# A two-layer perceiver kernel: masked keys of the first cross attention replaced by the mean of their block's unmasked keys, in place of mask products on the scores

## The chip, the cores and the metric

One core of one Trainium2 chip runs the whole program. The metric is device time in microseconds (us); the time before is 1705.82 us, the median of 3 runs (1701.45 to 1709.58).

## The reference, cut to what matters

Two layers, each of cross attention to a long context, self attention, and a mixture of experts. The change touches the first cross attention alone:

```python
q = _ln(q, qn_w, qn_b) * scale            # heads of 32 features, 16 heads, 512 queries
k = _ln(k, kn_w, kn_b)                    # 8192 keys
attn = jnp.einsum('bihd,bjhd->bhij', q, k)
attn = jnp.where(padding_mask[:, None, None, :], attn, -jnp.inf)
p = jax.nn.softmax(attn, axis=-1)
ctx = jnp.einsum('bhij,bjhd->bihd', p, v).reshape(b, s1, c)
```

The padding mask is true for a stretch at the end of the 8192 keys, so most blocks of 512 keys are wholly masked. With these inputs four of the sixteen blocks have unmasked keys (128 row maxima of 32 for each block in the trace), and only these are computed.

## The kernel before, in words

An attention has two halves. The first (`row_maxima`, lines 434 to 1183) goes over the active blocks, computes keys, values and scores, and keeps only the maximum of each row of scores for each head; keys and values are saved to DRAM. The second (`weighted_values`) computes the scores again, this time with the maximum subtracted, and the weighted values. A mask has to keep a masked key from winning a maximum in the first half, and from getting weight in the second. The change is to the first half of the first cross attention (`norm` and `whole` are true there, and nowhere else).

Its work on one block, for TensorE, is 16 *quads*, k = 0 to 15: one for each chunk c of four heads and each tile q of 128 queries. `quad` (L681 on) writes the scores of the four heads, 128 queries by 512 keys each, into two pairs of PSUM banks (`half` 0 and 1; a pair is two heads), by four products of 32 rows (L695) that lie in different row groups of the array. Then four products of 4 rows (L706) add the key mask: `PICK` is a matrix of ones in one row of each group, `KEYROW` holds 0 or -1e30 for each key, made by `key_bias` (L1049) at the head of the block. After the quad come two of the 32 products of the next block's keys (`project_keys`, L628) and this block's values (`project_values`, L670). In the last block there are only the values, one product for each quad, and no `spread`. (The trace counts each fp32 product twice.)

VectorE reduces each pair to two maxima (L1079, `tensor_reduce` of 128x1024), which frees it. There are three pairs, so that half h of a quad has to wait until the pair written three halves before has been reduced: the second half of a quad waits for the first half of the quad before. VectorE also normalises the keys of the next block: `invert` (L1025) takes reciprocals of the deviations, two after quad 9 and two after quad 10; TensorE spreads them over the heads' rows (`spread`, L681, after quad 11); `scale` (L1032) multiplies the keys `KW` by them, and ScalarE's `finish_keys` (L859) applies weight and bias of the norm and writes `KF`. `variances` (L649) stands after quad 8.

The queues are written out by hand, and every engine runs its own in order. ScalarE, near the end of a block (L949 to L956): values 0 and 1, `finish_keys` for chunks 0, 1, 2, values 2, four squares of a count of the second cross attention's mask (L836), values 3, `finish_keys` for chunk 3. SyncE, in `body` (L578 on), begins a block with `load_counted`, four loads of 1 MB of that second mask (L577), then `load_mask(i + 1)`, the key mask of the next block (L528, one 64 KB load, `KM`), then context and saves:

```python
wait_alone(sp, bias_ready, i + 1 + B)
load_mask(i + 1)
```

Each engine crosses from one block to the next through a loop with branches. GpSimd has nothing to do in this half but clear tiles for the second.

Of the kernel before, what the change touches and what calls it, by code (L numbers as in the profile page):

```python
# [14 lines left out]
P = 128  # L15
# [176 lines left out]
def active_blocks(nc, m, tag, count):  # L192
# [7 lines left out]
    class Parts:  # L200
        listed, listed_at = steps_done, 10
        weights, vectors, x = weights_loaded, vectors_loaded, x_loaded
# [12 lines left out]
        @staticmethod  # L215
        def vector(dve):
            v = nc.vector
            v.memset(m.CTL[:, :], 0).then_inc(steps_done, 1)
            v.memset(m.MINUS1[:, :], -1.0).then_inc(steps_done, 1)
            v.memset(m.ONEB[:, :], 1.0).then_inc(steps_done, 1)  # L220
            dve.wait_ge(keys_known, 16)
            v.tensor_reduce(F, m.KM[0:NB, 0:KB], AX.X, ALU.max).then_inc(steps_done, 1)
            dve.wait_ge(steps_done, 4)
            v.tensor_scalar(F, F, 0.0, None, ALU.is_gt).then_inc(steps_done, 1)
            dve.wait_ge(loaded, 16)
            v.tensor_copy(m.IDB[:, :], m.ident[:, :]).then_inc(steps_done, 1)
            v.tensor_copy(m.PICK[:, :], m.pick.to_broadcast([P, P])).then_inc(steps_done, 1)
            dve.wait_ge(products_done, 1)
            v.tensor_copy(POS, m.bank[2][0:NB, 0:1]).then_inc(steps_done, 1)
            dve.wait_ge(steps_done, 8)  # L230
# [4 lines left out]
            dve.wait_ge(steps_done, 10)  # L235

        @staticmethod
        def tensor(pe):
            t = nc.tensor
            pe.wait_ge(loaded, 16)  # L240
            pe.wait_ge(steps_done, 5)
            t.matmul(m.bank[2][0:NB, 0:1], m.upto[0:NB, 0:NB], F, start=True, stop=True).then_inc(products_done, 1)
            pe.wait_ge(steps_done, 9)
            t.matmul(m.bank[3][0:1, 0:1], m.ones[0:NB, 0:1], F, start=True, stop=True)
            t.matmul(m.bank[3][0:1, 1:1 + NB], m.index[0:NB, 0:1], LST, start=True, stop=True).then_inc(products_done, 1)
# [182 lines left out]
def row_maxima(nc, m, L):  # L428
# [25 lines left out]
    squared, inverse_ready, keys_final = m.sem(n + "_sq", norm), m.sem(n + "_rstd", norm), m.sem(n + "_kfull", dyn)  # L454
    maxima_done, mask_summed = m.sem(n + "_block", whole), m.sem(n + "_summed", L.row_mask)
    first_context = [m.sem(f"{n}_ctx_first{d}", norm) for d in range(DC)]
    values_stored = [m.sem(f"{n}_vstored{kb}", dyn) for kb in range(KT_)]
# [18 lines left out]

    VAR_AFTER, INVERSE_AFTER, SPREAD_AFTER = 8, (9, 10), 11

# [34 lines left out]
    class Parts:  # L513
        @staticmethod
        def sync(sp):
# [63 lines left out]
            def body(i):  # L579
                if counting:  # L580
                    load_counted(i)
                with sp.If(i + 1 < nb):
                    wait_alone(sp, bias_ready, i + 1 + B)
                    load_mask(i + 1)
# [23 lines left out]
        def tensor(pe):  # L608
# [65 lines left out]
            def spread(j, before, at):  # L674

                pe.wait_ge(inverse_ready, j * 4 + 4 + B)
                for half in range(2):
# [7 lines left out]
            def quad(i, at, k):  # L685
# [5 lines left out]
                for half in range(2):  # L691
                    pe.wait_ge(scores_taken, first_pair(i) + max(0, 2 * at - 2 + half))
                    for e in range(2):
                        g = 2 * half + e
                        last = t.matmul(m.pair[(2 * at + half) % 3][:, e, k0:k1], QF[rows(g), c, q * P:(q + 1) * P],  # L695
                                        m.KF[rows(g), c, k0:k1], start=True, stop=not whole)
                    if not whole:
                        last.then_inc(scores_ready, 1)
                if not whole:
                    return  # L700
                if k == 0:
                    pe.wait_ge(bias_ready, i + 1 + B)
                for half in range(2):
                    for e in range(2):
                        g = 2 * half + e
                        last = t.matmul(m.pair[(2 * at + half) % 3][:, e, :], m.PICK[rows(g, 4), :], m.KEYROW[rows(g, 4), :],  # L706
                                        start=False, stop=True)
                    last.then_inc(scores_ready, 1)
# [75 lines left out]
            if norm:  # L784

                pe.wait_ge(inverse_ready, 4 + B)
                for half in range(2):
# [38 lines left out]
        def scalar(act, at_last):  # L826
# [71 lines left out]
            if not begun:  # L898
# [29 lines left out]
            def body(i):  # L928
# [8 lines left out]
                with act.If(i + 1 < nb):  # L937
# [37 lines left out]
        def gpsimd(pool):  # L975
            g = nc.gpsimd
            if S:
                pool.wait_ge(q_projected, DC)
# [26 lines left out]
            if not norm:  # L1005

                def body(i):
                    with pool.If(i + 1 < nb):
                        copy_keys(i + 1, i)

                active_loop(pool, nb, body)
            return nb

        @staticmethod
        def vector(dve, at_last):
# [17 lines left out]

# [22 lines left out]
            def maxima(i, ahead):  # L1056
                if L.row_mask:
                    with dve.If(i >= 1):
                        row_bias(i)
                    dve.wait_ge(bias_ready, i + 1 + B)  # L1060
                elif dyn:
                    with dve.If(i >= 1):
                        key_bias(i)
                    dve.wait_ge(bias_ready, i + 1 + B)
                else:
                    dve.wait_ge(mask_loaded, 16)
                for at, k in enumerate(order if ahead else range(NS)):
                    if k == "spread":
                        scale(first_pair(i), at)
                        continue  # L1070
# [60 lines left out]

            if norm:
                for part in range(4):
                    invert(0, part)
# [5 lines left out]

                for half in range(2):
                    dve.wait_ge(scores_ready, B + half + 1)
                    s = m.KW[:, 2 * half:2 * half + 2, :]
                    v.tensor_tensor(s, s, m.pair[1 + half], ALU.mult).then_inc(scores_taken, 1)
                invert_query(0)
                scale_query(0)
                scale_query(1)
                key_bias(0)
                invert_query(2)
# [1026 lines left out]
def build(nc, d, out):  # L2176
    with ExitStack() as ctx:
# [43 lines left out]
        m.MASK = sb("MASK", [P, 2, NQ, KB])  # L2221
        m.MI, m.MB = m.MASK[:, 0].bitcast(I32), m.MASK[:, 1]
        m.MBK = m.BIG[:, 5 * DC * KB:5 * DC * KB + KT_ * T // 2].bitcast(BF16).rearrange("p (b n) -> p b n", n=T)

# [5 lines left out]
        m.CON, m.VT = sb("CON", [P, len(CONST), P]), sb("VT", [P, len(VEC), 4])  # L2230
        m.IDB, m.ONEB, m.PICK = (sb(x, [P, P], BF16) for x in ("IDB", "ONEB", "PICK"))
        m.KMW, m.KBIAS = sb("KM", [P, KB // 4], I32), sb("KBIAS", [P, KT_])
# [100 lines left out]
```

## Time and profile before

| what | value |
|---|---|
| median of 3 runs | 1705.82 us |
| lowest, highest run | 1701.45, 1709.58 us |
| profiled execution: its own time, read as its span | 1710.0 us |
| TensorE busy | 1608.9 us, 94% |
| VectorE busy | 1028.7 us, 60% |
| ScalarE busy | 522.1 us, 31% |
| GpSimd busy | 100.3 us, 6% |
| mean granted TensorE clock | 0.974 of full |
| first half of the first cross attention, by first score product of each block | 53.66, 116.46, 174.80, 231.97 us; ends at 277.62 us |

No time beyond the span is given for the profiled execution. Busy shares are means over stages with different limits. PE is TensorE (PEld its weight loads), DVE VectorE, ACT ScalarE, POOL GpSimd, SPq the queue of SyncE that issues DMAs.

### The profile page before, as it was taken

Reading aid. Unit: us, or ns where it says so; the run is one execution under the profiler, and the core shown is the slowest. Engines: PE = TensorE matmul, PEld = TensorE weight load, DVE = VectorE, ACT = ScalarE, POOL = GpSimd, SP = SyncE. Lnnn points to the kernel's source line nnn. Section 1 sums busy time; section 2 is a strip of 40 time slices with the busy share of each in tenths; the row PEclk is TensorE's granted clock in tenths of the full one; section 3 lists DMA queues with packets and bytes.
Section 4 is the critical chain, followed back from the end, with each engine's and each line's share of the span. In section 5 each row is a group of like instructions: output and inputs, shape, how many; then the busy total and the mean of one; then the engine's idle time right before and its main releaser. Section 6 shows DMA issues by size and latency. Waiting matters only on the chain. (4 is left out here: it accounts for less than half of the span.)

```text
span 1710.0 us, 27863 instructions
## 1 busy us (share of the span) xinstructions
PE 1608.9 (94%) x9460; PEld 758.6 (44%) x9471; DVE 1028.7 (60%) x1681; ACT 522.1 (31%) x781; POOL 100.3 (6%) x82
## 2 busy tenths in 40 slices
PE   7999999999899889999999899998999899989997
PEld 3333333222343376666665433332222244467775
DVE  6677777999746551111111599998979945652223
ACT  3434434878413310000000211114658612200000
POOL 0200001000002010000000320000300001010001
PEclk9899998999999989999999999998999999989999
DMA  4442332211067967666661423210412021239996
GB/s 167 149 151 110 143 141 82 64 51 37 0 133 124 197 235 256 235 233 225 235 235 57 152 91 117 74 67 32 158 39 74 0 86 32 100 122 336 325 327 228
DMA packets 73420, 240.28 MB, mean 141 GB/s; under 512 B 7328, under 2 KB 20528, under 8 KB 54032
## 3 DMA queue, kind: packets, MB, share of 16 engines
q1 hardware_dynamic: 64752, 220.42, 39.8%
q10 hardware_dynamic: 6048, 10.69, 1.7%
q0 software_dynamic: 2560, 8.39, 1.5%
q8 instruction: 36, 0.59, 0.1%
q14 instruction: 24, 0.20, 0.0%
HBM read 214.04 MB, written 35.91 MB: 146 GB/s over the span
## 5 line engine op out<-in xcount | busy, mean ns | idle before, releaser
L1564 ACT ACTIVATE BIG<-banks 128x1024 f32<-128x1024 f32 (+5 forms) x320 | 282.1, 934 | 122.5 <-PE banks L1510 121.7
L1086 DVE CUSTOM_DVE_ANT_0 BIG<-banks,MASK,MX 128x512 bf16<-128x512 f32 (+5 forms) x384 | 228.9, 656 | 61.8 <-issue 38.3
L2106 PEld LDWEIGHTS banks<-KF,BIG 128*128 128x128 f32 x1792 | 227.0, 191 | 14.1 <-issue 14.1
L2106 PE MATMUL banks<-KF,BIG 128*128 128x160 f32 (+1 forms) x1792 | 229.2, 289 | 2.6 <-DVE KF L1824 2.0
L2134 PE MATMUL banks<-BIG,PB 128*128 128x512 f32 x448 | 202.9, 600 | 0.0
L695 PE MATMUL banks<-KF,XN 32*128 32x512 f32 (+4 forms) x1280 | 188.8, 609 | 11.4 <-DVE MX L1086 3.8
L1503 PE MATMUL banks<-XN,KF 32*128 32x512 f32 (+4 forms) x1280 | 187.9, 614 | 7.4 <-ACT BIG L1564 5.3
L1615 DVE TENSOR_TENSOR PB<-PB,BIG 128x2048 f32<-128x2048 f32 (+5 forms) x78 | 165.7, 2124 | 22.6 <-ACT BIG L1564 20.2
L1079 DVE TENSOR_REDUCE MXW<-banks 128x2 f32<-128x1024 f32 x128 | 150.3, 1216 | 44.6 <-PE banks L706 43.4
L1470 PE MATMUL banks<-BIG,V 128*32 128x512 f32 (+4 forms) x1280 | 160.4, 570 | 5.0 <-issue 2.6
L2134 PEld LDWEIGHTS banks<-BIG,PB 128*128 128x128 f32 x448 | 81.5, 190 | 113.1 <-issue 112.9
L670 PE MATMUL banks<-WV,XNT 128*128 128x512 f32 x256 | 126.2, 617 | 0.0
L695 PEld LDWEIGHTS banks<-KF,XN 32*128 32x128 f32 x1280 | 59.3, 186 | 144.9 <-DVE MX L1086 71.6
L628 PE MATMUL banks<-CT,WK 128*128 128x512 f32 x224 | 115.4, 643 | 4.5 <-DVE WK L420 4.5
L1503 PEld LDWEIGHTS banks<-XN,KF 32*128 32x128 f32 x1280 | 63.7, 187 | 124.9 <-issue 75.4
L2019 ACT ACTIVATE PS<-banks 128x512 f32<-128x512 f32 x20 | 11.9, 597 | 332.7 <-PE banks L2134 299.9
L1893 DVE TENSOR_TENSOR PB<-V,banks 128x640 f32<-128x640 f32 x32 | 26.3, 821 | 118.6 <-ACT V L2005 114.5
L1615 DVE TENSOR_TENSOR PS<-PS,BIG 128x2048 f32<-128x2048 f32 (+5 forms) x39 | 82.9, 2126 | 8.5 <-ACT BIG L1564 7.6
L1888 DVE TENSOR_SCALAR V<-banks 128x512 f32<-128x512 f32 x24 | 16.6, 691 | 115.4 <-PE banks L2106 113.6
L866 ACT ACTIVATE V<-banks 128x512 f32<-128x512 f32 x40 | 23.9, 597 | 197.3 <-PE banks L670 197.3
L1615 DVE TENSOR_TENSOR BIG<-BIG 128x2048 f32<-128x2048 f32 (+5 forms) x39 | 80.4, 2062 | 5.0 <-ACT BIG L1564 4.3
L670 PEld LDWEIGHTS banks<-WV,XNT 128*128 128x128 f32 x256 | 43.7, 189 | 70.1 <-issue 60.5
(296 smaller groups left out, 1468.1 us busy)
## 6 DMA issues: line engine op xcount, KB each, us to landing
BIG<-in_L0f_w SPq DMA_DIRECT2D x64, 1024.0 KB, 4.8
BIG<-in_L1f_w SPq DMA_DIRECT2D x48, 1024.0 KB, 5.7
BIG<-in_mask_q SPq DMA_DIRECT2D x16, 1024.0 KB, 8.0
k_saved<-KF SPq DMA_DIRECT2D x32, 256.0 KB, 2.7
CT<-in_ctx SPq DMA_DIRECT2D x6, 1024.0 KB, 4.8
XNT<-in_ctx SPq DMA_DIRECT2D x6, 1024.0 KB, 6.4
v_saved<-V SPq DMA_DIRECT2D x24, 256.0 KB, 2.4
KF<-k_saved SPq DMA_DIRECT2D x24, 256.0 KB, 3.3
```

The source lines that it names most:

```text
L628: last = t.matmul(bank[:, n0:], m.WK[:, d, x * P:(x + 1) * P], KSRC[:, d, n0:], start=d == 0, stop=d == DC - 1)
L670: last = t.matmul(value_bank(kb), tokens[:, d, kb * P:(kb + 1) * P], m.WV[:, d, :], start=d == 0, stop=d == DC - 1)
L695: last = t.matmul(m.pair[(2 * at + half) % 3][:, e, k0:k1], QF[rows(g), c, q * P:(q + 1) * P], m.KF[rows(g), c, k0:k1], start=True, stop=n ...
L1079: v.tensor_reduce(m.MXW[:, H * q + h:H * q + h + 2], pair, AX.X, ALU.max).then_inc(scores_taken, 1)
L1086: last = v.tensor_tensor_reduce(m.JUNK[:, 2 * half + e, k0:k1], pair[:, e, k0:k1], bias, 1.0, mx, ALU.add, ALU.max, mx)
L1470: last = t.matmul(m.bank[6 + c % 2][rows(g), q0:q1], m.V[:, kt[k], HD * h:HD * h + HD], m.PE_[:, s % NP, g, q0:q1], start=k == 0, stop=k = ...
L1503: t.matmul(out(g), m.KF[rows(g), c, ks], m.QF[rows(g), c, q0:q1], start=not biases, stop=False)
L1564: a.activation(m.PE_[:, s % NP, 2 * half:2 * half + 2, q0:q1], m.pair[(2 * s + half) % 3][:, :, q0:q1], ACT.Exp).then_inc(exp_ready, 1)
L1615: v.tensor_tensor(dst, dst, m.PE_[:, s % NP, :, q0:q1], ALU.add).then_inc(sum_taken, 1)
L1893: v.tensor_tensor(out, ex, hidden[k % 2], ALU.mult).then_inc(hidden_copied, 1)
L2106: last = t.matmul(out, W1[k][:, d, f * P:(f + 1) * P], XE[:, d, :], start=d == 0, stop=d == DC - 1)
L2134: last = t.matmul(YB, HS[:, 4 * k + f, 0:P], W2[k][:, f, :], start=k + f == 0, stop=(k == NF - 1 and f == 3), skip_group_check=True)
```

## The change

In this half a masked key now gets the mean of the unmasked keys of its block as its key. A score against a mean of keys is the mean of their scores, so that it can't exceed their maximum. To get there:

- the deviations' reciprocals are multiplied by the mask (a fifth step of `invert`), so that masked keys come out of `scale` as zeros;
- `scale` is now four `tensor_tensor_reduce` of 128x512, which give the sums of the keys as well, and one small step makes them means;
- GpSimd's `fill_keys` adds (mask) x (mean) to each chunk in two steps with a wait between; `finish_keys` waits for it;
- `key_mask` (after quad 3, for the next block) makes the mask, the count of keys and its reciprocal; it needs the key mask of the next block in SBUF;
- SyncE's wait before `load_mask` is on the fifth inverse; ScalarE's order at the start and at a block's end is changed;
- `key_bias`, `PICK` and the four mask products of each quad go; `scores_ready` is raised after each half's own products.

```diff
@@ row_maxima
+    MASK_AFTER, VAR_AFTER, INVERSE_AFTER, SPREAD_AFTER = 3, 8, (9, 10), 11
+    INVERTED = 5
+    NKEYS, KSUMS, KMEANS = m.small[:, 248:249], m.small[:, 250:250 + DC], m.small[:, 254:254 + DC]
@@ sync, body
                 if counting:
                     load_counted(i)
                 with sp.If(i + 1 < nb):
-                    wait_alone(sp, bias_ready, i + 1 + B)
+                    if whole:
+                        wait_alone(sp, inverse_ready, i * INVERTED + INVERTED + B)
+                    else:
+                        wait_alone(sp, bias_ready, i + 1 + B)
                     load_mask(i + 1)
@@ tensor, spread
-                pe.wait_ge(inverse_ready, j * 4 + 4 + B)
+                pe.wait_ge(inverse_ready, j * INVERTED + INVERTED + B)
@@ tensor, quad
                         last = t.matmul(m.pair[(2 * at + half) % 3][:, e, k0:k1], QF[rows(g), c, q * P:(q + 1) * P],
-                                        m.KF[rows(g), c, k0:k1], start=True, stop=not whole)
-                    if not whole:
-                        last.then_inc(scores_ready, 1)
-                if not whole:
-                    return
-                if k == 0:
-                    pe.wait_ge(bias_ready, i + 1 + B)
-                for half in range(2):
-                    for e in range(2):
-                        g = 2 * half + e
-                        last = t.matmul(m.pair[(2 * at + half) % 3][:, e, :], m.PICK[rows(g, 4), :], m.KEYROW[rows(g, 4), :],
-                                        start=False, stop=True)
+                                        m.KF[rows(g), c, k0:k1], start=True, stop=True)
                     last.then_inc(scores_ready, 1)
@@ scalar, finish_keys
-                act.wait_ge(scores_taken, (B if free is None else spread_pair(free)) + c // 2 + 1)
+                act.wait_ge(keys_filled, j * DC + c + 1 + B)
@@ scalar, at the start
                 finish_keys(0, 0, None)
+                squared_query(2)
                 finish_keys(0, 1, None)
-                finish_keys(0, 2, None)
-                squared_query(2)
-                finish_keys(0, 3, None)
                 finish_query(0)
                 finish_query(1)
+                finish_keys(0, 2, None)
                 squared_query(3)
+                finish_keys(0, 3, None)
                 query_roots(2)
@@ scalar, body
-                        for c in range(DC - 1):
-                            finish_keys(i + 1, c, i)
+                        finish_keys(i + 1, 0, i)
+                        finish_keys(i + 1, 1, i)
                     values(i, 2)
+                    if norm:
+                        finish_keys(i + 1, 2, i)
                     count_one(3)
                     values(i, 3)
@@ gpsimd
+            def fill_keys(j):
+
+                wait_alone(pool, mean_ready, j + 1 + B)
+                for c in range(DC):
+                    wait_alone(pool, keys_filled, j * DC + c + B)
+                    g.tensor_scalar(m.FILL, m.MASKED, KMEANS[:, c:c + 1], None, ALU.mult).then_inc(filling, 1)
+                    wait_alone(pool, filling, j * DC + c + 1 + B)
+                    g.tensor_tensor(m.KW[:, c, :], m.KW[:, c, :], m.FILL, ALU.add).then_inc(keys_filled, 1)
@@ vector
+                if part == INVERTED - 2:
+                    dve.wait_ge(bias_ready, j + 1 + B)
+                    dve.wait_ge(inverse_ready, j * INVERTED + INVERTED - 1 + B)
+                    v.tensor_tensor(m.RSTD, m.RSTD, m.KM[:, 0:KB], ALU.mult).then_inc(inverse_ready, 1)
-            def scale(before, at):
+            def scale(j, before, pairs):
 
                 for half in range(2):
-                    dve.wait_ge(scores_ready, before + 2 * at + half + 1)
-                    s = m.KW[:, 2 * half:2 * half + 2, :]
-                    v.tensor_tensor(s, s, m.pair[(2 * at + half) % 3], ALU.mult).then_inc(scores_taken, 1)
+                    dve.wait_ge(scores_ready, before + half + 1)
+                    for e in range(2):
+                        c = 2 * half + e
+                        last = v.tensor_tensor_reduce(m.KW[:, c, :], m.KW[:, c, :], pairs[half][:, e, :], 1.0, 0.0,
+                                                      ALU.mult, ALU.add, KSUMS[:, c:c + 1])
+                    last.then_inc(scores_taken, 1)
+                dve.wait_ge(scores_taken, before + 2)
+                v.tensor_scalar(KMEANS, KSUMS, NKEYS, None, ALU.mult).then_inc(mean_ready, 1)
-            def key_bias(i):
-
-                if not isinstance(i, int):
-                    dve.wait_ge(scores_taken, first_pair(i))
-                dve.wait_ge(mask_loaded, i * 16 + 16 + B)
-                v.tensor_scalar(m.KEYROW, m.KM[:, 0:KB], m.mask_factor, m.mask_offset, ALU.mult, ALU.add).then_inc(bias_ready, 1)
+            def key_mask(j):
+
+                dve.wait_ge(mask_loaded, j * 16 + 16 + B)
+                dve.wait_ge(keys_filled, j * DC + B)
+                v.tensor_scalar(m.MASKED, m.KM[:, 0:KB], -1.0, 1.0, ALU.mult, ALU.add).then_inc(keys_counted, 1)
+                v.tensor_reduce(NKEYS, m.KM[:, 0:KB], AX.X, ALU.add).then_inc(keys_counted, 1)
+                dve.wait_ge(keys_counted, 2 * j + 2 + B)
+                v.reciprocal(NKEYS, NKEYS).then_inc(bias_ready, 1)
@@ vector, maxima
-                elif dyn:
-                    with dve.If(i >= 1):
-                        key_bias(i)
-                    dve.wait_ge(bias_ready, i + 1 + B)
+                    if ahead and norm and k == MASK_AFTER:
+                        key_mask(i + 1)
```

At the start `key_mask(0)` stands before the first four reciprocals, `key_bias(0)` goes, and `fill_keys(0)` stands ahead of GpSimd's clearing of tiles.

## Rows read from the trace of the kernel before

**Rows 1.** The page: busy time, share of the span and instructions of each engine.

```profile
PE 1608.9 (94%) x9460; PEld 758.6 (44%) x9471; DVE 1028.7 (60%) x1681; ACT 522.1 (31%) x781; POOL 100.3 (6%) x82
```

**Rows 2.** Stretches: length, PE, PEld, DVE, ACT, POOL busy (count), clock, DMA share, GB/s.

```profile
174.80:231.97 57.17, 55.53 (x272) 18.87 (x272) 43.76 (x41) 24.86 (x52) 0.00 (x0) 1.00 0.35 130
116.46:174.80 58.34, 57.19 (x272) 19.37 (x272) 43.54 (x40) 24.05 (x51) 0.00 (x0) 0.97 0.39 145
53.66:116.46 62.80, 61.47 (x276) 20.23 (x276) 47.49 (x42) 26.38 (x53) 7.47 (x5) 0.92 0.38 140
231.97:277.60 45.63, 43.11 (x224) 15.38 (x224) 38.44 (x34) 17.21 (x41) 0.00 (x0) 0.93 0.27 103
```

**Rows 3.** Timeline, last quads of block 2: start, duration, instruction, idle before and releaser.

```profile
167.81 1.14 PE L695 MATMUL banks<-KF,XN 32*128 32x512 f32 x8
...
171.01 1.14 PE L695 MATMUL banks<-KF,XN 32*128 32x512 f32 x8
171.97 0.40 PE L706 MATMUL banks<-BIG,PICK 4*128 4x512 bf16 x4
172.30 1.98 PE L670 MATMUL banks<-WV,XNT 128*128 128x512 f32 x4
172.39 2.35 DVE L1079 TENSOR_REDUCE MXW<-banks 128x2 f32<-128x1024 f32 x2 [0.85 <-PE banks L706]
...
174.80 1.14 PE L695 MATMUL banks<-KF,XN 32*128 32x512 f32 x8 [0.52 <-DVE MXW L1079]
```

**Rows 4.** Timeline, block 3: key mask, second quad, mask load, tenth quad.

```profile
176.45 0.55 DVE L1049 TENSOR_SCALAR BIG<-KM,CON 128x512 bf16<-128x512 uint8 x1 [1.45 <-issue]
...
179.30 1.14 PE L695 MATMUL banks<-KF,XN 32*128 32x512 f32 x8
...
181.75 0.34 SPq L528 DMA_DIRECT2D KM<-in_keymask  x1
...
205.91 1.14 PE L695 MATMUL banks<-KF,XN 32*128 32x512 f32 x8
```

**Rows 5.** Timeline of PE in the second cross attention's first half, no mask products.

```profile
1000.62 1.14 PE L695 MATMUL banks<-KF,XN 32*128 32x512 f32 x8
1001.70 1.98 PE L670 MATMUL banks<-WV,XNT 128*128 128x512 f32 x4
1003.61 1.14 PE L695 MATMUL banks<-KF,XN 32*128 32x512 f32 x8
```

**Rows 6.** Timeline, block 4: key mask, second quad, end.

```profile
233.78 0.55 DVE L1049 TENSOR_SCALAR BIG<-KM,CON 128x512 bf16<-128x512 uint8 x1 [1.60 <-issue]
...
236.96 2.09 PE L695 MATMUL banks<-KF,XN 32*128 32x512 f32 x8
...
277.62 0.22 DVE L1098 TENSOR_TENSOR MX<-MX,MXW 128x64 f32<-128x64 f32 x1
```

**Rows 7.** DMA issues by line: count, KB each, median us to landing, 170 to 200 us.

```profile
BIG<-in_mask_q SPq DMA_DIRECT2D x4, 1024.0 KB, 8.5
...
KM<-in_keymask SPq DMA_DIRECT2D x1, 64.0 KB, 11.9
```

**Rows 8.** Lines by shape (busy, mean ns, idle before); of L1342 its least, median, most ns.

```profile
L1032 DVE TENSOR_TENSOR BIG<-BIG,banks 128x1024 f32<-128x1024 f32 x6 | 7.0, 1212 | 0.0
L222 DVE TENSOR_REDUCE small<-KM 16x1 f32<-16x512 uint8 x1 | 0.7, 674 | 1.4 <-DMA KM<-in_keymask 1.4
L1086 DVE CUSTOM_DVE_ANT_0 BIG<-banks,MASK,MX 128x512 bf16<-128x512 f32 x256 | 175.6, 749 | 12.9 <-PE banks L695 11.8 <-DVE MASK L1041 1.1
L1001 POOL COPY KF<-BIG 128x512 f32<-128x512 f32 x12 | 7.4, 613 | 125.8 <-PE banks L695 125.8
L1342 POOL TENSOR_TENSOR X<-X,RAROWS x16: 1255/1918/3322, 282.8 to 1452.9; 128x512 f32<-128x512 f32 x16
```

**Rows 9.** Timeline of the start: the last query chunk read, the first quad.

```profile
50.18 0.69 ACT L876 ACTIVATE BIG<-banks,VT 128x512 f32<-128x512 f32 x1 [0.54 <-PE banks L640]
...
53.66 2.09 PE L695 MATMUL banks<-KF,XN 32*128 32x512 f32 x8 [1.11 <-issue]
```

More of the change, by code:

```diff
@@ L200, in active_blocks @@
     class Parts:
-        listed, listed_at = steps_done, 10
+        listed, listed_at = steps_done, 9
         weights, vectors, x = weights_loaded, vectors_loaded, x_loaded
@@ L226, in vector @@
             v.tensor_copy(m.IDB[:, :], m.ident[:, :]).then_inc(steps_done, 1)
-            v.tensor_copy(m.PICK[:, :], m.pick.to_broadcast([P, P])).then_inc(steps_done, 1)
             dve.wait_ge(products_done, 1)
             v.tensor_copy(POS, m.bank[2][0:NB, 0:1]).then_inc(steps_done, 1)
-            dve.wait_ge(steps_done, 8)
+            dve.wait_ge(steps_done, 7)
             v.tensor_scalar(LST, m.ramp[0:NB, 1:NB + 1], POS, F, ALU.is_equal, ALU.mult).then_inc(steps_done, 1)
@@ L234, in vector @@
             v.tensor_copy(m.CTL[0:1, count:count + 1 + NB], m.bank[3][0:1, 0:1 + NB]).then_inc(steps_done, 1)
-            dve.wait_ge(steps_done, 10)
+            dve.wait_ge(steps_done, 9)
         @staticmethod
@@ L242, in tensor @@
             t.matmul(m.bank[2][0:NB, 0:1], m.upto[0:NB, 0:NB], F, start=True, stop=True).then_inc(products_done, 1)
-            pe.wait_ge(steps_done, 9)
+            pe.wait_ge(steps_done, 8)
             t.matmul(m.bank[3][0:1, 0:1], m.ones[0:NB, 0:1], F, start=True, stop=True)
@@ L455, in row_maxima @@
     maxima_done, mask_summed = m.sem(n + "_block", whole), m.sem(n + "_summed", L.row_mask)
+    keys_counted, mean_ready, filling, keys_filled = (m.sem(n + x, whole) for x in ("_counted_keys", "_kmean", "_kfilling", "_kfilled"))
     first_context = [m.sem(f"{n}_ctx_first{d}", norm) for d in range(DC)]
@@ L475, in after_quad @@
         return todo[k * len(todo) // n:(k + 1) * len(todo) // n] if k >= 0 else []
-    VAR_AFTER, INVERSE_AFTER, SPREAD_AFTER = 8, (9, 10), 11
+    MASK_AFTER, VAR_AFTER, INVERSE_AFTER, SPREAD_AFTER = 3, 8, (9, 10), 11
+    INVERTED = 5
+    NKEYS, KSUMS, KMEANS = m.small[:, 248:249], m.small[:, 250:250 + DC], m.small[:, 254:254 + DC]
     order = list(range(NS))
@@ L784, in tensor @@
             if norm:
-                pe.wait_ge(inverse_ready, 4 + B)
+                pe.wait_ge(inverse_ready, INVERTED + B)
                 for half in range(2):
@@ L976, in gpsimd @@
             g = nc.gpsimd
+            def fill_keys(j):
[5 more added lines that the diff above has]
+                    g.tensor_tensor(m.KW[:, c, :], m.KW[:, c, :], m.FILL, ALU.add).then_inc(keys_filled, 1)
+            if whole:
+                fill_keys(0)
             if S:
@@ L1011, in gpsimd, with body @@
                 active_loop(pool, nb, body)
+            if whole:
+                def body(i):
+                    with pool.If(i + 1 < nb):
+                        fill_keys(i + 1)
+                active_loop(pool, nb, body)
             return nb
@@ L1060, in maxima @@
                     dve.wait_ge(bias_ready, i + 1 + B)
-                elif dyn:
-                    with dve.If(i >= 1):
-                        key_bias(i)
-                    dve.wait_ge(bias_ready, i + 1 + B)
-                else:
+                elif not dyn:
                     dve.wait_ge(mask_loaded, 16)
@@ L1068, in maxima @@
                     if k == "spread":
-                        scale(first_pair(i), at)
+                        scale(i + 1, first_pair(i) + 2 * at, [m.pair[(2 * at + half) % 3] for half in range(2)])
                         continue
@@ L1132, in vector @@
             if norm:
+                key_mask(0)
                 for part in range(4):
@@ L1139, in invert_query @@
                     v.reciprocal(s, s).then_inc(q_inverse, 1)
[L1141 to L1144, printed above, removed]
+                scale(0, B, [m.pair[1 + half] for half in range(2)])
                 invert_query(0)
@@ L1147, in vector @@
                 scale_query(1)
-                key_bias(0)
                 invert_query(2)
@@ L2222, in build @@
         m.MI, m.MB = m.MASK[:, 0].bitcast(I32), m.MASK[:, 1]
+        m.MASKED, m.FILL = m.MASK[:, 1, 0, :], m.MASK[:, 1, 1, :]
         m.MBK = m.BIG[:, 5 * DC * KB:5 * DC * KB + KT_ * T // 2].bitcast(BF16).rearrange("p (b n) -> p b n", n=T)
@@ L2230, in build @@
         m.CON, m.VT = sb("CON", [P, len(CONST), P]), sb("VT", [P, len(VEC), 4])
-        m.IDB, m.ONEB, m.PICK = (sb(x, [P, P], BF16) for x in ("IDB", "ONEB", "PICK"))
+        m.IDB, m.ONEB = (sb(x, [P, P], BF16) for x in ("IDB", "ONEB"))
         m.KMW, m.KBIAS = sb("KM", [P, KB // 4], I32), sb("KBIAS", [P, KT_])
```

## The prediction

> **What bounds the kernel now.** The page first: TensorE is busy 94% of the span, VectorE 60%, GpSimd 6% [rows 1]. That is a mean over stages; this change lies in one of them, the four blocks between 53.66 and 277.6 us, so I cut the trace there [rows 2]. In blocks 1 to 3 TensorE is busy nearly throughout (55.53 of 57.17 us in block 3) and VectorE about 76%. In block 4, with half the side products, VectorE is busy 38.44 of 45.63 us.
>
> Then the timeline of one quad [rows 3]. Score products start every 3.20 us (167.81, 171.01). In a period stand the scores, the mask products 0.96 us later, the value products 0.33 us after that. VectorE needs 2.35 us for the two reductions (2.42 with their waits) and idles 0.85. So TensorE sets the period in blocks 1 to 3, with only 0.8 us of room beside it. At the end of a block the next block's first product waits for the last reduction (174.80).
>
> The head of a block [rows 4]: VectorE makes the key mask at 176.45, the mask products wait for it, and the second quad starts at 179.30, 4.50 us after the first instead of 3.20. Last, the DMA queue: the key mask for the next block is issued at 181.75 behind four loads of 1 MB, and lands 11.9 us after issue [rows 4, 7]. Today nobody needs it before the next block, over 38 us later.
>
> **Mask products out.** 0.33 us from the first mask product to the value products [rows 3] would make 16 x 3 x 0.33 = 15.8 us in blocks 1 to 3. But the same loop runs in the second cross attention without them, with a period of 2.99 us (1000.62 to 1003.61), and there the value products start 1.08 us after the scores, not 0.96 [rows 5]. A quad saves 0.215 us, so I take that: 0.12 us of the drain of the scores was hidden by the mask products. The Trainium skill, "TensorE: Matmul & The Clock Gate", Back-to-back issue gap, gives a product of 512 columns about 0.216 us, and its Part 3 says that products in different row groups overlap; by that four mask products cost about 0.22 us together, 10.4 us over 48 quads. That agrees with rows 5 and not with the 0.33 us of rows 3. In the stretch from quad 9 on VectorE rules (below), so only quads 1 to 8 count: 8 x 0.215 = **1.7 us a block**, blocks 1 to 3.
>
> **The head of a block.** No mask is made there, so the second quad can follow after 2.99 us: 4.50 - 2.99 = 1.5 us in block 3. Block 2 has the same work and is 1.17 us longer, at a clock of 0.97 instead of 1.00 [rows 2]; I give back that too: 2.7 us. Block 1's head is in the start below.
>
> **From quad 9 to the next block.** This takes 26.06 us in block 3 (205.91 to 231.97) [rows 2, 4] and is a chain through VectorE: reductions, four reciprocals, `scale`. Added to the chain: RSTD x mask, about 0.61 us (half of the 1.212 us that `scale` takes for twice as many elements); four 0.749 us steps for two of 1.212 us, 0.57 us more [rows 8]; the means, 0.2 us (like the 0.22 us of L1098 [rows 6]). 1.4 us, less the mask products of the last two quads (0.4): **0.9 to 1.0 us lost a block**.
>
> **Fill and finish.** GpSimd is idle here, so its own time is free. A chunk takes a one-source step, nearest row 0.613 us, and an add, 1.255 to 3.322 us [rows 8]; I take 0.6 + 1.26 + 0.2 for the waits = 2.1 us, since in this stretch VectorE reads mostly PSUM. Four chunks: 8.4 us after the means, while quads 12 to 15 and the wait for the last reduction leave 10.5 us. Hidden, with 2 us of cover. What is late is `finish_keys` of chunk 3: behind it in SyncE's queue stand its save, the four 1 MB loads and the key mask. I put them 1 us later. At the upper end (3.9 us a chunk) the cover is gone; that is a rival.
>
> **`key_mask`.** On VectorE: 0.55 us (as L1049), 0.67 us (L222), a small reciprocal and waits, together 1.5 us [rows 4, 8]. With its data there, 1.0 us fits in the room that the 2.99 us period leaves over two quads, and 0.5 us is lost. But it needs the next block's mask **after quad 3**. Count from the block's first product, block 3: the load is issued 181.75 - 174.80 = 6.95 us in, lands 11.9 us later, at 18.85, and with the 1 us above at **19.8 us**. VectorE is there at 3 x 2.99 + 1.3 (scores to reduction, as 171.01 to 172.39 [rows 3]) + 2.4 = **12.7 us**. It then stands 7.1 us, with the reductions of quad 4 queued behind it; `key_mask` ends at 21.3, the first half of quad 4 is reduced at 22.5. TensorE waits for that before the second half of quad 5, due at 15. Quad 6 starts at 22.6 + 0.95 + 1.91 = 25.5 instead of 17.9: **7.5 us lost, in blocks 2 and 3**. There is no other work to fill it, since TensorE's queue is in order. SyncE's changed wait itself costs nothing: SyncE comes to it from the four loads, when that inverse is long done.
>
> After standing 7 us the clock will be at its lower level for a while. Block 2 now has 0.97 x 58.34, or 3.5 us at half speed, worth 1.75 us, after a stop of TensorE far shorter [rows 2]; block 4 has 0.93 x 45.63, worth 3.2 us. I take 1.8 us for each stall; the ends are 0 and 3.2.
>
> In block 1 the mask load goes out early, before the slow first quads are over, and by the same count (landing about 18 us in, quad 3 reduced about 18 us in, because quads 0 and 1 run at 1.2 GHz, as the 2.09 us group of products shows [rows 9]) I expect no stall there beyond the 0.5 us.
>
> **Block 4.** No `key_mask`, no spread. VectorE sets the pace: it may reduce from about 1.8 us in (where it made the mask, 233.78) and needs 16 x 2.42 = 38.7 us, so 40.5 us instead of 45.63: 5.1 us at most [rows 2, 3, 6]. The second quad now runs at half speed (2.09 us) [rows 6]; if the head still does that, 2 us remain. Taken: **3.5 us**.
>
> **The start.** `key_mask(0)` delays the reciprocals by 1.5 us, which hides behind query products; `scale` and the means are 0.8 us longer before the query's reciprocals; ScalarE must wait for the third filled chunk before it reads the last query chunk (now at 50.18, I get 51.7), and the first quad (53.66) needs that [rows 9]. 1.5 us late, less 0.4 for quad 0's mask products: **1.1 us lost**. The later order of `finish_keys`, the clearing of tiles by GpSimd 10 us later (needed only in the second half) and the dropped cast of PICK cost nothing: the block's quads cover them; without that cover GpSimd's clearing would cost its 1.8 us steps.
>
> **The sum.** Block 1 and start: 1.7 - 0.5 - 0.9 - 1.1 = -0.8. Block 2: 2.7 + 1.7 - 0.9 - 7.5 - 1.8 = -5.8. Block 3: 1.5 + 1.7 - 0.9 - 7.5 - 1.8 = -7.0. Block 4: +3.5. Together 10.1 us slower: 1710.0 to 1720.1 us for the profiled execution. That one is 0.25% over the median of the runs, 1705.82, so for the median 1715.9 us. 0.5% (8.5 us) is about what a measurement of this kernel can tell from no change.
>
> **Rivals.**
> (a) The mask is there in time, because the small load doesn't wait for the four large ones once it is wanted. Then blocks 2 and 3 lose 0.5 us each instead of 9.3: 3.0 + 1.8 + 3.5 - 0.8 = 7.5 us faster, 1698.3, and up to 1696.7 with block 4's 5.1 us. It decides at the landing: under about 13 us from the block's first product it holds. Against it: the 64 KB load's 11.9 us is longer than the 8.5 us of the 1 MB loads issued before it [rows 7]. For it: nobody waited for that load, so nothing shows its landing in use. Chance 0.12.
> (b) The stall is there but partly made good: ScalarE and SyncE run no later than before (landing at 18.85), the clock stays up, block 4 gives all 5.1 us. Per stall 6.5 us instead of 9.3: 10.1 - 5.6 - 1.6 = 3 us slower, 1708.7. For it: the cover estimates are rough. Chance 0.2.
> (c) The fill is late: 3.9 us a chunk, if the add is slowed as L1342's worst case is [rows 8]. Chunk 3 and the last values come 4 to 5 us after TensorE wants them, at each of three block ends, and the mask load slips as much in two: about 20 us on top, 1736. The Trainium skill, "GPSIMD Engine Reference", Specifications, says that GpSimd shares its SBUF interface with VectorE where that has two SBUF inputs; no row of this stretch shows GpSimd beside such a step. Chance 0.06.
> (d) Forecast as summed, 1715.9: chance 0.62. Its own range, from the ends of the clock (0 to 3.2 each), the head of block 4 and a microsecond or two in landing: 1710 to 1721.
>
> **How the numbers follow.** Over 1714.3: all of (c), 0.44 of (d): 0.5. Under 1697.3: not quite half of (a), and a little for gains I don't see: 0.08. Within: the rest, 0.42. The range goes down past (b) to 1702 and up to 1722; (a) and (c) are left out.
>
> **What would show it.** In the profile after: VectorE idle 6 to 8 us before L1049's successor in `key_mask`, released by the load of KM, in blocks 2 and 3 and not in 1; TensorE idle 6 to 7 us in quad 5, released by a reduction; blocks 2 and 3 near 64 us, block 4 near 42; quads apart 2.99 us in quads 1 to 3. The forecast is wrong if KM lands before VectorE asks, or if quads 12 to 15 wait for keys or values.

## The result, and the profile after

The changed kernel takes 1723.76 us (median of 4 runs, 1722.72 to 1725.07), before 1706.49 us over the runs made beside it: ratio 1.0093, 95% interval 1.0065 to 1.0121. It is slower by 16 to 17 us. The forecast was 10.1 us slower, 1715.9 us, with a range to 1722. The direction and the main cause, the wait for the mask, hold; the fill, forecast as hidden, was not; and the time lies 1.8 us outside the range.

The profiled execution after took 1722.72 us and spans 1720.9 us. First the four blocks, cut at each block's first score product as in [rows 2]: the stretches of the kernel after (length, PE, PEld, DVE, ACT, POOL busy, clock, DMA share, GB/s).

```profile
57.76:117.49 59.73, 58.20 (x213) 18.41 (x213) 49.79 (x53) 23.05 (x46) 18.99 (x14) 0.92 0.31 115
117.49:183.82 66.33, 57.38 (x208) 18.36 (x209) 45.09 (x50) 24.54 (x51) 10.99 (x9) 0.92 0.34 128
183.82:249.50 65.68, 58.07 (x209) 18.76 (x209) 45.30 (x51) 24.88 (x52) 11.33 (x9) 0.92 0.31 113
249.50:289.15 39.65, 36.49 (x160) 12.05 (x160) 36.88 (x33) 20.05 (x49) 1.75 (x2) 1.00 0.35 132
```

The first quad starts 4.1 us later than before (57.76 for 53.66). Block 1 is 3.1 us shorter, block 2 8.0 us longer, block 3 8.5 us longer, block 4 6.0 us shorter. That ends the half 11.5 us later (289.15 for 277.62); behind it 0.6 us come back.

Where the time went in block 2 is in the timeline (start, duration, instruction, idle before and releaser), here around quads 3 to 7, and in the last line the same stop in block 3:

```profile
127.19 0.34 SPq L530 DMA_DIRECT2D KM<-in_keymask  x1
...
128.12 1.14 PE L700 MATMUL banks<-KF,XN 32*128 32x512 f32 x8
...
131.11 1.14 PE L700 MATMUL banks<-KF,XN 32*128 32x512 f32 x8
...
134.09 1.13 PE L700 MATMUL banks<-KF,XN 32*128 32x512 f32 x4
...
138.95 0.43 DVE L1072 TENSOR_SCALAR MASK<-KM 128x512 f32<-128x512 uint8 x1 [7.29 <-DMA KM<-in_keymask]
139.29 0.68 DVE L1073 TENSOR_REDUCE small<-KM 128x1 f32<-128x512 uint8 x1
140.00 0.16 DVE L1075 RECIPROCAL small<-small 128x1 f32<-128x1 f32 x1
140.10 4.63 DVE L1101 TENSOR_REDUCE MXW<-banks 128x2 f32<-128x1024 f32 x4
...
141.38 2.08 PE L700 MATMUL banks<-KF,XN 32*128 32x512 f32 x4 [6.16 <-DVE MXW L1101]
...
143.39 3.78 PE L633 MATMUL banks<-CT,WK 128*128 128x512 f32 x4
...
147.10 2.05 PE L700 MATMUL banks<-KF,XN 32*128 32x512 f32 x8
...
151.00 1.14 PE L700 MATMUL banks<-KF,XN 32*128 32x512 f32 x8
...
205.44 0.43 DVE L1072 TENSOR_SCALAR MASK<-KM 128x512 f32<-128x512 uint8 x1 [5.63 <-DMA KM<-in_keymask]
```

Quads without trouble are 2.99 us apart (128.12, 131.11, 134.09). VectorE comes to `key_mask` after quad 3 and stands 7.29 us for the load of KM, issued at 127.19 and landed 11.7 us later. The first half of quad 5 is written at 134.09; its second half, at 141.38, has waited 6.16 us for the reduction of quad 4. From there TensorE runs at the 1.2 GHz level: 2.08, 3.78 and 2.05 us where 2.4 GHz takes 1.14, 1.98 and 1.14. In block 3 VectorE stands 5.63 us. Before, no engine waited for this load in these blocks.

The second loss is at the head of the block, again in the timeline after:

```profile
116.00 0.81 ACT L853 ACTIVATE KF<-BIG,VT 128x512 f32<-128x512 f32 x1 [1.92 <-POOL BIG L981]
116.09 1.56 POOL L979 TENSOR_SCALAR MASK<-MASK,small 128x512 f32<-128x512 f32 x1 [0.21 <-POOL BIG L981]
116.72 0.70 ACT L830 ACTIVATE BIG<-BIG,MINUS 128x512 int32<-128x512 int32 x1
...
117.49 1.14 PE L700 MATMUL banks<-KF,XN 32*128 32x512 f32 x8 [0.88 <-DVE MXW L1101]
...
117.84 1.27 POOL L981 TENSOR_TENSOR BIG<-BIG,MASK 128x512 f32<-128x512 f32 x1 [0.18 <-POOL MASK L979]
...
119.54 0.57 ACT L860 ACTIVATE V<-banks 128x512 f32<-128x512 f32 x1
...
120.25 1.98 PE L633 MATMUL banks<-CT,WK 128*128 128x512 f32 x4 [1.62 <-ACT V L860]
...
122.16 1.14 PE L700 MATMUL banks<-KF,XN 32*128 32x512 f32 x8
```

ScalarE reads values 3 only at 119.54: it had waited 1.92 us for filled chunk 2 (L853) and then did the four squares of L830, and TensorE waits 1.62 us for it. In the page's manner, the two steps of the fill by shape, in the first 330 us (busy, mean ns, idle before):

```profile
L979 POOL TENSOR_SCALAR MASK<-MASK,small 128x512 f32<-128x512 f32 x16 | 25.0, 1565 | 191.5 <-DVE small L1056 189.1 <-POOL BIG L981 2.5
...
L981 POOL TENSOR_TENSOR BIG<-BIG,MASK 128x512 f32<-128x512 f32 x16 | 20.2, 1265 | 3.3 <-POOL MASK L979 3.3
```

A chunk takes 1.57 + 1.27 us and 0.4 us of waits between the steps, 3.2 us in all, and the four 12.8 us.

### The profile page after: what moved, and what is told of

The parts are those of the page before. It is cut to its first block and busy times, and to the rows that moved or that the text cites. A ratio compares the mean times of both kernels' runs of the same rounds, so it can differ in the third digit from the quotient of the medians.

```text
span 1720.9 us, 27544 instructions
## 1 busy us (share of the span) xinstructions
PE 1603.7 (93%) x9214; PEld 753.3 (44%) x9215; DVE 1033.8 (60%) x1720; ACT 522.4 (30%) x781; POOL 146.2 (8%) x114
## 5 line engine op out<-in xcount | busy, mean ns | idle before, releaser
L700 PE MATMUL banks<-KF,XN 32*128 32x512 f32 (+4 forms) x1280 | 193.4, 611 | 21.8 <-DVE MXW L1101 12.6
L633 PE MATMUL banks<-CT,WK 128*128 128x512 f32 x224 | 119.5, 663 | 8.2 <-DVE WK L419 4.6
L1909 DVE TENSOR_SCALAR V<-banks 128x512 f32<-128x512 f32 x24 | 16.6, 692 | 119.1 <-PE banks L2127 118.1
L633 PEld LDWEIGHTS banks<-CT,WK 128*128 128x128 f32 x224 | 41.5, 204 | 82.8 <-issue 69.8
```

Of the source, the lines that this page charges most:

```text
L633: last = t.matmul(bank[:, n0:], m.WK[:, d, x * P:(x + 1) * P], KSRC[:, d, n0:], start=d == 0, stop=d == DC - 1)
```

## The experiments

Theory: VectorE's wait for the mask load, with the clock after it, is the loss; the late fill adds a smaller part. Rivals: the fill is the loss; or the load is slow wherever it stands. Below, blocks and the stage's end are measured as above, from each kernel's own profile; "ratio" is to the kernel before, run on the same chip.

### The same kernel again

> The kernel before, once more, for the spread of one kernel's times and of its stages. The profiled execution of before spans 1710.0 us, more than any of its timed runs. If its first half of the first cross attention (53.66 to 277.62 us) is typical, then this profile shows the same block lengths within 0.5 us (62.8, 58.3, 57.2, 45.7) and the surplus lies after 280 us; if the surplus is in these blocks, they come out shorter here. Time within 0.3% of before either way.

Ratio 1.002 (1.0001 to 1.0039), where 1 is true: a ratio from three rounds can be 0.2% off, and its interval can just miss 1. The span was 1703.5 us. The stretches of this second profile of before:

```profile
53.47:113.79 60.32, 56.84 (x276) 19.31 (x277) 47.52 (x42) 26.36 (x53) 7.47 (x5) 1.00 0.39 145
113.79:172.17 58.38, 57.21 (x273) 19.30 (x273) 43.56 (x40) 24.07 (x51) 0.00 (x0) 0.97 0.39 145
172.17:229.34 57.17, 55.54 (x273) 18.92 (x274) 43.77 (x41) 24.87 (x52) 0.00 (x0) 1.00 0.35 130
229.34:273.65 44.31, 41.63 (x224) 15.39 (x224) 38.45 (x35) 17.20 (x41) 0.00 (x0) 0.96 0.28 107
```

Blocks 2 and 3 repeat to 0.1 us, their clock too. Block 1 is 2.5 us shorter at clock 1.00 instead of 0.92, block 4 1.3 us shorter at 0.96 instead of 0.93 [rows 2]. So the execution on which I forecast spent 4.0 us more in this stage than another execution of the same kernel, in the blocks where its clock was lower. Against this profile the changed kernel ends the half 15.5 us later (289.15 for 273.65), not 11.5. But this profile isn't a typical one either: its run, 1705.24 us, was the fastest of ten (median 1709.92).

### `key_mask` after quad 7

```diff
-    MASK_AFTER, VAR_AFTER, INVERSE_AFTER, SPREAD_AFTER = 3, 8, (9, 10), 11
+    MASK_AFTER, VAR_AFTER, INVERSE_AFTER, SPREAD_AFTER = 7, 8, (9, 10), 11
```

> The changed kernel with key_mask after quad 7 instead of quad 3, when the key mask has landed by its trace. Theory (the wait for the mask load is the loss): blocks 2 and 3, 66.3 and 65.7 us in the changed kernel, lose the stop and the half-speed clock after it, 10.0 and 8.3 us, and come to 56.5 to 57.5 us; about 18 us under the changed kernel, so 1705 us, no difference to before. Rival (the loss is the late fill, values and start): both blocks keep over 62 us and the time stays at 1718 or more.

1704.18 us, ratio 0.999 (0.9968 to 1.0011). The two stretches of blocks 2 and 3:

```profile
119.50:173.27 53.77, 52.60 (x209) 17.26 (x209) 45.30 (x51) 22.02 (x44) 9.56 (x7) 1.00 0.39 148
173.27:232.02 58.75, 55.73 (x208) 18.11 (x209) 45.29 (x51) 27.92 (x60) 13.06 (x10) 0.94 0.37 135
```

12.6 and 6.9 us less than in the changed kernel, where 10.0 and 8.3 were expected; VectorE waits for no load in these blocks. The median is 19.6 us under the changed kernel's, and the stage ends 18.9 us earlier (270.25). One number, which sets where VectorE waits, gives back the whole loss against before: the theory holds, and the rival that the fill is the main loss falls. Block 3 has 5.0 us more than block 2 for the same work: 1.93 us are a wait for values at its head, the rest goes with its clock of 0.94.

### The mask load ahead of the large ones

```diff
-                if counting:
-                    load_counted(i)
                 with sp.If(i + 1 < nb):
...
                     load_mask(i + 1)
+                if counting:
+                    load_counted(i)
+                with sp.If(i + 1 < nb):
                     wait_alone(sp, k_projected, i * NK + NK + DC + B)
```

> The changed kernel with the load of the key mask issued ahead of the four 1 MB loads of a block, key_mask still after quad 3. Theory (the mask lands last because it is issued last): it lands in 2 to 6 us and before VectorE asks; the same 17 to 18 us back, 1706 us, with 0.5 us a block left for key_mask inside the narrow room after quad 3. Rival (the load is slow wherever it stands, since all loads share the same engines): it still lands some 12 us after issue, now about 3.5 us sooner in the block, the stop shrinks to 3 to 4 us and the time is about 1715 us.

1703.18 us, ratio 0.9966 (0.9946 to 0.9987). The load lands 3.1 to 5.3 us after issue (three loads), where in the changed kernel the same three took 10.2 to 11.6, and VectorE never waits for it; `key_mask` stands where it stood. So the landing time was made by the four loads issued before it, and the rival falls. By the medians 20.6 us come back; by the stage's end (274.32) only 14.8, since the profiled run was 4.4 us over its median and its block 3 took 60.39 us at a clock of 0.92. Two edits with nothing in common, one on VectorE's side and one on SyncE's, each take the wait away and give back the loss against before, which leaves little room for another cause.

### The fill left out

```diff
@@ finish_keys
-                act.wait_ge(keys_filled, j * DC + c + 1 + B)
+                act.wait_ge(scores_taken, (B if free is None else spread_pair(free)) + c // 2 + 1)
@@ key_mask
-                dve.wait_ge(keys_filled, j * DC + B)
@@ gpsimd
-            if whole:
-                fill_keys(0)
...
-                        fill_keys(i + 1)
```

Masked keys are left at zero.

> The changed kernel without GpSimd's fill: masked keys stay zero before the norm's weight and bias, and finish_keys waits for scale as it did before. Theory: the wait for the mask stays, and what goes is the fill's share: the first quad 2.5 us earlier (1.6 us late instead of 4.1), and the waits of TensorE for values at the heads of blocks 2 to 4 (1.6, 1.9, 1.9 us) with the mask load 2 us earlier; 7 to 9 us under the changed kernel, about 1716 us. Rival (the fill is the main loss): 1708 us or less, with VectorE's wait for the mask gone or under 3 us.

1711.5 us, ratio 1.0023 (1.0001 to 1.0045), 12 us under the changed kernel by the medians, 8.5 us by the stage's end (280.67). Against the 7 to 9 us expected that is more by the medians and within by the stage's end. In its profile VectorE still waits 14.0 us for KM in all, 6.7 us the longest. So the fill costs 30% (by the stage's end) to 45% (by the medians) of the gap to the version without either, below, and the mask wait is there without it.

### Both out

> The changed kernel with key_mask after quad 7 and without GpSimd's fill (masked keys stay zero): both costs out. Theory: the two costs add, the fill's share being that which no_fill showed (some 8 to 12 us), less where the stop hid it; heads of blocks without a wait for values, first quad at 54.9 us; 1697 us, some 9 us under before and 7 under mask_after_7. Rival (with the wait for the mask gone the fill is hidden): the same time as mask_after_7, 1704 us, within 2 us.

1696.25 us, ratio 0.9904 (0.9875 to 0.9933). By the stage's end: changed kernel 289.15; without the fill 8.5 us less, without the wait 18.9 less, without both 28.7 less (260.46). The two add up within 1.3 us. The rival, that the fill would be hidden once the wait is gone, falls.

### The queue of ScalarE in another order

The complete change, with `key_mask` after quad 7 and

```diff
@@ body
-                    count_one(3)
                     values(i, 3)
+                    count_one(3)
@@ at the start
                 finish_query(1)
-                finish_keys(0, 2, None)
                 squared_query(3)
-                finish_keys(0, 3, None)
+                finish_keys(0, 2, None)
                 query_roots(2)
+                finish_keys(0, 3, None)
```

> The changed kernel, complete, with key_mask after quad 7, and ScalarE's queue in another order: values 3 ahead of the four squares of the count at a block's end, and at the start the last query chunk read ahead of finish_keys for chunk 2 and the query roots ahead of chunk 3. Theory: what the slow fill (3.2 us a chunk) costs is what stands behind it in ScalarE's queue, so TensorE's waits for values at the heads of blocks 2 to 4 (1.6 to 1.9 us each) go and the first quad comes near 55.2 us instead of 58: 1697 us, as late_no_fill. Rival (the keys themselves are late): no change to mask_after_7, with TensorE waiting for finish_keys instead.

1695.31 us, ratio 0.992 (0.9892 to 0.9947), and once more:

> The kernel of late_reordered once more. Theory: no half-speed clock in its blocks 2 to 4, so that they repeat within 0.1 us (53.8, 53.7, 38.2), and 0.991 to 0.993 of before, 28 us under the changed kernel. Rival (its clock was luck): one of the three blocks comes out 2 us or more longer.

1699.8 us, ratio 0.9934 (0.9913 to 0.9955). The stretches of the first of the two:

```profile
55.78:115.23 59.45, 58.28 (x212) 18.42 (x212) 49.25 (x53) 23.50 (x45) 21.41 (x15) 0.92 0.35 130
115.23:169.00 53.77, 52.59 (x208) 17.21 (x208) 45.29 (x51) 24.90 (x52) 11.36 (x9) 1.00 0.43 158
169.00:222.72 53.72, 52.54 (x208) 17.16 (x208) 45.29 (x51) 24.87 (x52) 11.33 (x9) 1.00 0.37 138
222.72:260.95 38.23, 37.04 (x160) 12.24 (x160) 36.79 (x34) 19.95 (x49) 1.77 (x2) 1.00 0.36 137
```

In the second profile blocks 2 to 4 are 53.77, 53.72 and 38.24 us, as expected; the ratio of 0.9934 is a little over the 0.991 to 0.993 expected, and the time is 25.5 us under the changed kernel's on the same chip, not 28. In neither profile does TensorE wait for values or for `finish_keys` in blocks 2 to 4. With the fill complete the stage ends at 260.95 us, without it at 260.46. So the 12.8 us of GpSimd cost about 0.5 us in themselves; what they cost was the values and the query chunk that stood behind `finish_keys` in ScalarE's queue. Which of the moves gives how much was not tested one by one. The first quad came at 55.8 us, 0.6 later than expected. This version is 0.7 to 0.8% under before and beats both kernels.

### The gain alone

Before, without the mask products and TensorE's wait for the mask (maxima are then taken over masked keys too):

```diff
-                                        m.KF[rows(g), c, k0:k1], start=True, stop=not whole)
...
-                        last = t.matmul(m.pair[(2 * at + half) % 3][:, e, :], m.PICK[rows(g, 4), :], m.KEYROW[rows(g, 4), :],
-                                        start=False, stop=True)
+                                        m.KF[rows(g), c, k0:k1], start=True, stop=True)
```

> The kernel before without the four mask products of each quad and TensorE's wait for the mask (the first half of the first cross attention then takes its maxima over masked keys too); VectorE still makes the mask row at the head of a block. This is the gain of the change without any of its costs. Theory: quads 2.99 us apart instead of 3.20, the head of a block 1.5 us shorter, block 3 near 53.5 us instead of 57.2, block 4 near 40 instead of 44.3 to 45.7; 14 to 16 us under before, 1692 us. Rival (a quad saves the 0.33 us between the first mask product and the next product): quads 2.87 us apart, block 3 near 52 us.

1690.22 us, ratio 0.9872 (0.983 to 0.9913), 19 us under before by the medians, more than the 14 to 16 expected; against the second profile of before the stage ends 16.8 us earlier (256.82). TensorE's timeline in block 3:

```profile
173.83 1.14 PE L695 MATMUL banks<-KF,XN 32*128 32x512 f32 x8
174.90 1.98 PE L628 MATMUL banks<-CT,WK 128*128 128x512 f32 x4
176.82 1.14 PE L695 MATMUL banks<-KF,XN 32*128 32x512 f32 x8
```

The period is 2.99 us and the products after the scores start 1.07 us behind them, as [rows 5] had it and not [rows 3]. Blocks 2 and 3 are 53.78 and 53.45 us. The reordered kernel's blocks 2 and 3 come within 0.3 us of that with all the new work in them.

### The wait alone

Before, with one wait more:

```diff
+                    if ahead and norm and k == 3:
+                        dve.wait_ge(mask_loaded, (i + 1) * 16 + 16 + B)
```

> The kernel before with nothing but one wait added: VectorE waits, after quad 3, for the load of the next block's key mask. Theory: the wait alone costs time. VectorE is there about 14.7 us after a block's first product, the load lands at 18.9 in blocks 2 and 3, so a stop of some 4 us in each, 3 us of it for TensorE, and up to 1.8 us more for the clock after it; block 1 has little or none; 6 to 9 us over before, 1714 us. Rival (VectorE's idle 0.8 us a quad and the pairs of banks swallow a stop of 4 us): under 2 us over before.

1712.54 us, ratio 1.001 (0.9992 to 1.0029): by the timed runs the cost isn't clear of nothing, it is less than the 6 to 9 us expected, and the rival's "under 2 us" isn't excluded. By the stage's end (281.00 for 273.65) it is 7.4 us. Its profile shows the mechanism, with two stops of the same length and different ends. The stretches from the stop's end in blocks 2 and 3:

```profile
133.31:142.00 8.69, 8.69 (x36) 3.10 (x40) 5.79 (x5) 3.74 (x9) 0.00 (x0) 0.80 0.00 0
...
195.04:204.00 8.96, 8.96 (x27) 2.93 (x28) 4.52 (x4) 3.26 (x8) 0.00 (x0) 0.62 0.00 0
```

VectorE stood 4.22 and 4.30 us, as expected, TensorE only 1.71 and 1.79 us, where 3 were expected. Block 2 became 2.4 us longer than in the second profile of before (60.76 for 58.38), block 3 6.2 us (63.37 for 57.17): behind the second stop the clock was at its lower level for more of the time.

### The changed kernel again

> The changed kernel once more, on one chip with the reordered one. Theory (the profiled execution of before was a slow one in its blocks 1 and 4, 62.8 and 45.7 us against 60.3 and 44.3 in its second profile, and the changed kernel's was an ordinary one): this profile ends the first half within 2 us of the 289.2 us it had, and the timed ratio to before is 1.008 to 1.010 again. Rival (the changed kernel's profile was the lucky one): blocks 2 and 3 or the part behind them come out over 3 us longer here.

1725.32 us, ratio 1.0091 (1.0063 to 1.0119). Its stage ends at 287.02 us, 2.1 us earlier than in the first profile (2 was the bound), blocks 60.72, 63.64, 65.48 and 39.67. The changed kernel's profile was thus an ordinary one. Of the profiles of before one was slow and one fast against the median. In block 1 it is the first that stands apart: from 53.5 to 70 us its clock was 0.69, while in the second profile, in `before_wait_only` and in `before_no_products` it was 1.00.

## Why the prediction was right and wrong, point by point

Two steps of the prediction failed: the fill, which was to be hidden, and the last step, from the profiled execution to the median. The points in turn.

**The wait for the mask** came as written: VectorE stood 7.29 us in block 2 (7.1 forecast) and 5.63 in block 3, none in block 1. The landing time was read off the kernel before, where nobody waited for it, from the issue times and the queue ahead of the load. That the stop in block 2 fits to 0.2 us is partly luck: from the block's first product, VectorE came after 14.2 us (12.7 forecast) and the mask after 21.5 (19.8 forecast), both late by about as much. Rival (a) is what `mask_load_first` makes true, by moving the load, not otherwise.

**The clock behind the stop** was mis-sized in part. From quad 1 to quad 7 block 2 took 28.84 us and block 3 26.37 us, where six periods are 17.9: 10.9 and 8.5 us lost. The forecast was 7.5 + 1.8 = 9.3 for each. In block 3 the stop was 1.7 us shorter, since the head had already held TensorE up: the block's second quad came 6.49 us after its first. By an estimate from the clocks, 0.60 over 141.38:151.00 and 0.66 over 207.87:216.68 with TensorE busy throughout, the clock cost 3.8 and 3.0 us where 1.8 was forecast, which leaves 7.1 and 5.5 us for the stops.

**The fill** failed as a step. "A chunk takes a one-source step, nearest row 0.613 us": it took 1.565 us, more than the add with two sources (1.265). A chunk was 3.2 us, not 2.1. "Hidden, with 2 us of cover" was wrong: the means' step starts at 105.81 and the last add ends 119.1, behind the next block's first product at 117.49. TensorE waited for values at three heads (1.62, 1.94, 1.93 us), and the first quad was 4.1 us late, not 1.5. The prediction's own sign, quads 12 to 15 waiting for keys or values, missed it: the wait came one quad later, at the next block's head. Without the fill (`no_fill`) the ratio to before was 1.0023, some 1710.4 us by the median of before here, well inside the range. In direction that is rival (c), which I gave 0.06, at about half its size and from another cause: the add ran at its fastest. The upper end of the range had left (c) out.

**Mask products and the head of a block**: 2.99 us and 0.215 us a quad, right. The head of 2.99 us came only where the fill didn't hold up the values (115.23 to 118.22 in the reordered kernel); in the changed kernel's first profile the heads were 4.67 and 6.49 us. **From quad 9 on**: 0.9 us lost was forecast. In block 2 of the changed kernel it took 25.85 us (157.97 to 183.82) for 26.06 before, 0.2 us gained. `before_no_products` splits this: the same stretch takes 24.99 us there (139.28 to 164.27), so that the mask products gave 1.07 us, not 0.4, and the added work cost 0.86, not 1.4. A part of the latter is that the four steps of `scale` start 0.61 us apart, not 0.749. **Block 4**: 3.5 forecast, 6.0 measured against the first profile of before, 4.7 against the second.

**The sum** was 10.1 us and the two profiles differ by 10.9. That is luck in part, with errors that cancel: block 2 lost 8.0 us (5.8 forecast) and block 3 8.5 (7.0), block 4 gained 6.0 (3.5), and 0.6 us came back behind the stage.

The other step that failed is **the level**: "1710.0 to 1720.1 us for the profiled execution. That one is 0.25% over the median of the runs, 1705.82, so for the median 1715.9 us." The changed kernel's profiled run lists both numbers, 1722.72 us for a span of 1720.9, so there are 1.8 us around a span, and by that estimate before's profiled execution took about 1711.8 us, 5.3 over its median of 1706.49. The whole gap of 17.3 us is 10.9 between the profiles, 5.3 by which before's was slow, and 1.0 by which the changed kernel's was fast. I took the profiled execution's span for its time, and carried the difference over to the median as if all of a slow execution's surplus would stay in the changed kernel: 4.2 us off, where the changed kernel's median lay 2.9 us over the span of its profile. A part of the surplus lay in this stage, the 4.0 us of blocks 1 and 4. The reading is that the change took their place, so that its savings there were savings on time that a median run doesn't spend. That is argued, not shown: the second profile of before, which lacks them, was the fastest of its ten runs. Two profiles of each kernel end the stage at 277.62 and 273.65 before, and 289.15 and 287.02 after, 12.5 us apart on average. Where the rest of the difference of the medians lies, no run shows. The chances, with 0.5 for slower by over 0.5%, leaned the right way.

Open: why the clock goes to its lower level behind one gap and not behind another of the same length was not settled. The parts behind the stage differ by up to 13 us between profiles of unchanged code (1427.0 to 1439.9 us from the stage's end), which no run here explains.

## What to carry to other kernels

Before a consumer is moved forward, look up when its data lands today, not only when the consumer stops: a load that nobody waits for shows its price in no list of waits, but its issue and landing are in the trace. If a small load is wanted early, issue it ahead of the large ones on its queue. When an engine's queue gains a wait, what matters is what stands behind it; here moving a few calls ahead of the wait made a 12.8 us chain all but free. And a baseline's profile is one execution: compare its own time with the median and its clock by stage with a second profile before taking savings from it, and the second one's time with the median too.

## What was not expected of the hardware

- On GpSimd a product of 128x512 with one scalar for each partition took 1.565 us (16 times, 1.564 to 1.569), the add of two tensors of the same shape 1.265 us, a copy 0.613 us [rows 8]. The step with one tensor wasn't cheaper there than the one with two.
- VectorE's `tensor_tensor_reduce` of 128x512 takes 0.68 us, but the next starts 0.61 us after it began (169.95, 170.55, 171.16 in the changed kernel); the 0.08 us read of the sum stands beside the start of the next.
- The same kernel ran the first 16.5 us of block 1 at a clock of 0.69 in one execution and 1.00 in another (the stretches 53.66:70.00 and 53.47:70.00). The Trainium skill, "TensorE: Matmul & The Clock Gate", Part 1, calls the point of the change run-variable and the ramp's penalty under 1% of a typical kernel's span. The trace agrees. But the 4.0 us between the two executions in this stage, of 1706, are 0.23%, nearly half of the 0.5% that the prediction took for what a measurement of this kernel can tell from no change.
